# A two-layer graph network on one core: node blocks turned by transposing DMAs instead of by TensorE

## The reference

```
agg(h)  = segment_sum(h[src], dst) / max(degree, 1)
block 1:  h  = relu([h0, agg(h0)] @ W1 + b1)             # 128+128 -> 256
          y  = log_softmax([h, agg(h)] @ W2 + b2)        # 256+256 -> 128
block 2:  h3 = relu(agg(h2) @ Wl0.T + bl0 + h2 @ Wr0.T)  # 128 -> 256
          h4 = relu(agg(h3) @ Wl1.T + bl1 + h3 @ Wr1.T)  # 256 -> 256
          y  = relu(h4 @ Wa.T + ba) @ Wb.T + bb          # -> 128
```

## Time and profile before

| | |
|---|---|
| median of three runs | 587.96 us |
| the profiled execution: time / span | 587.56 us / 585.7 us |
| TensorE matmul busy | 544.2 us (93%) |
| VectorE / ScalarE busy | 225.0 / 202.9 us |
| phase 1, steps of chunks 1 to 6 | 68 to 204 us |
| phase 2 / phase 3 / phase 4 | from 204 / 276 / 372 us |
| TensorE's clock, mean over the span | 0.992 |

### The profile page before, as it was taken

How to read it: one execution, slowest core, us unless ns; L and a number is a source line. 1 busy time by engine, 2 the same in 40 slices (tenths; PEclk the granted TensorE clock), 3 DMA queues, 4 the chain that set the end, 5 groups by cost and what they waited for, 6 DMA issues and landing times.

```text
span 585.7 us, 9420 instructions
## 1 busy us (share of the span) xinstructions
PE 544.2 (93%) x3078; PEld 291.5 (50%) x3078; DVE 225.0 (38%) x500; ACT 202.9 (35%) x368; POOL 24.7 (4%) x36
## 2 busy tenths in 40 slices
PE   1367999999999999999999999999999999999996
PEld 0244655555554654445455555644545445454555
DVE  6899959577775217667411111110000001010001
ACT  1688858567664304455422222200000010100011
POOL 4410000000000000110100000000000000000000
PEclk9997999999999999999999999999999999999999
DMA  3800103010010124333121111232011212111011
GB/s 94 196 1 1 38 1 117 2 36 17 17 35 17 24 70 112 90 90 77 39 76 53 52 52 39 67 117 52 19 35 39 49 35 52 35 35 52 17 32 30
DMA packets 31372, 29.47 MB, mean 50 GB/s; under 512 B 4894, under 2 KB 30879, under 8 KB 31215
## 3 DMA queue, kind: packets, MB, share of 16 engines
q1 hardware_dynamic: 29622, 27.91, 17.6%
q10 hardware_dynamic: 1561, 0.84, 0.6%
q0 software_dynamic: 160, 0.33, 0.2%
HBM read 19.68 MB, written 9.39 MB: 50 GB/s over the span
## 4 chain that ended last, share of the span: by engine, by line
PE 87%; DVE 5%; ACT 3%; DMA 2%; issue 2%; POOL 1%; ACTq 0%; SPq 0%; DVEq 0%; POOLq 0%
PE ps L1036 54%; PE ps L1053 22%; PE ps L990 6%; PE ps L1308 2%; DVE hs_b L493 2%; PE ps L1046 1%; PE ps L1270 1%; DMA hs_b<-self_d 1%; DMA adj<-key_d,adj 1%; ACT adj L1490 1%; POOL adj L1375 1%; PE ps L1242 1%; DVE adj L1426 1%; DMA adj<-in_dst_dram 0%; ACT adj L844 0%
## 5 line engine op out<-in xcount | busy, mean ns | idle before, releaser
L1036 PE MATMUL ps<-adj,hs_b 125*128 (+2 forms) x1050 | 203.6, 351 | 0.0
L1036 PE MATMUL ps<-adj,hs_a 125*128 (+2 forms) x700 | 158.5, 353 | 0.0
L1036 PEld LDWEIGHTS ps<-adj,hs_b 125*128 125x128 f16 x1050 | 96.3, 97 | 103.9 <-issue 6.6
L493 DVE TENSOR_TENSOR hs_b<-iota,hs_b 128x1024 f16<-128x1024 f16 x150 | 95.4, 685 | 27.9 <-PE ps L990 26.9
L844 ACT ACTIVATE adj<-ps 125x500 f32 (+2 forms) x150 | 80.0, 544 | 22.8 <-PE ps L990 16.6
L990 PE MATMUL ps<-hs_b 128*128 128x125 f16 x625 | 68.5, 233 | 20.7 <-DVE hs_b L493 13.1
L990 PEld LDWEIGHTS ps<-hs_b 128*128 128x128 f16 x625 | 46.5, 103 | 65.7 <-DVE hs_b L493 34.4
L1036 PEld LDWEIGHTS ps<-adj,hs_a 125*128 125x128 f16 x700 | 58.5, 98 | 38.8 <-issue 5.4
L975 ACT ACTIVATE actT<-ps,col 128x500 f32<-128x500 f32 (+1 forms) x14 | 8.9, 633 | 148.0 <-PE ps L1053 148.0
L791 DVE TENSOR_TENSOR hs_a<-ps,hs_a 125x512 f32<-125x512 f32 (+1 forms) x7 | 4.4, 634 | 128.9 <-PE ps L1308 128.9
L1053 PE MATMUL ps<-aggT,wts 128*128 128x500 f32 (+1 forms) x112 | 44.6, 540 | 0.4 <-ACT aggT L957 0.4
(11 more groups left out here) (150 smaller groups left out, 356.4 us busy)
## 6 DMA issues: line engine op xcount, KB each, us to landing
invc<-inv_d SPq DMA_DIRECT2D x24, 250.0 KB, 3.3
h_d<-actT SPq DMA_DIRECT2D x6, 500.0 KB, 3.1
wts<-h_d SPq DMA_DIRECT2D x6, 500.0 KB, 4.0
self_d<-hs_b SPq DMA_DIRECT2D x6, 250.0 KB, 2.1
hs_b<-self_d SPq DMA_DIRECT2D x6, 250.0 KB, 3.5
hs_b<-in_x_dram SPq DMA_DIRECT2D x6, 250.0 KB
x_d<-hs_b SPq DMA_DIRECT2D x6, 250.0 KB
hs_a<-x_d SPq DMA_DIRECT2D x6, 250.0 KB
```

Of the source, the lines that this page charges most:

```text
L493: last = nc.vector.tensor_tensor(onehots[slot], iota2.unsqueeze(1).to_broadcast(shape), keys[:, ds(g * 4, 4), :].unsqueeze(2).to_broadcast ...
L1036: last = nc.tensor.matmul(acc[:, 0:n], hs[:, ds(s * (2 * w) + part * w + h * 128, 128)], adj[0:P, ds(c * (S * C) + s * n, n)], start=(isin ...
```

## The change

- Rows of the first normalization are stored to DRAM (`hs_d1`) in five pieces of 625 rows (`rows_out`), the rows of h2 chunk by chunk (`hs_d3`).
- The own rows of a full chunk come back turned: `turn_own` issues two transposing DMAs (high halves, low halves) of 512 rows x 128. VectorE adds the two (`own_sum`). `own1` and `own3` are left for chunk 6 only.
- z of a full chunk: ScalarE writes the high half as f16 (turned layout), VectorE the low half (`z_low`), SyncE stores both to `z_d`, waits, and issues four transposing DMAs of 256 rows that write `hs_b`. h3 of chunks 0 to 4 goes the same way: two ScalarE copies, two VectorE subtractions, two stores to `h16_d`, four transposing DMAs of 512 rows. `turn1` is left for chunk 6, `turn3` for chunks 5 and 6; `low` and `high` likewise.
- Phase 2 now begins on `p1_zin` (the transposed z of five chunks, of the sixth before tile 20), phase 4 on `p3_in`.
- A memset of `zT` on GpSimd, and pads zeroed on VectorE. The branch for inputs that don't fit (not taken here) gets shared semaphores.

```diff
 # SyncE
+            def turn_own(ph, c, hd, into):
+                for k in range(2):
+                    sp.dma_start_transpose(into[k], hd[ds(c * C, 512), k * D:(k + 1) * D]).then_inc(sem(f"p{ph}_hT"), 16)
             load_inv("p1_", 0, True)
+            if not slow:
+                rows_out(sp, 3, S // PIECE)          # pieces 0 to 2 are stored before the branch
+                sp.wait_ge(sem("h0_rows"), 16 * (S // PIECE))
+                turn_own(1, 0, hs_d1, turned1)
             def step1(c, full, nxt):
                 sp.wait_ge(sem("p1_agg_out"), c + 1)
                 if nxt is not None:
                     load_inv("p1_", c + 1, nxt)
                 if not slow and isinstance(c, int) and c == 0:
                     store_weights()
+                if not slow and nxt:
+                    sp.wait_ge(sem("p1_h0T"), c + 1)
+                    turn_own(1, c + 1, hs_d1, turned1)
                 sp.wait_ge(sem("p1_self"), c + 1)
                 sp.dma_start(self_d[...], selfT[...])
+                if not slow and full:
+                    sp.wait_ge(sem("p1_zlo"), c + 1)
+                    sp.dma_start(z_d[...], zboth...).then_inc(sem("p1_z_out"), 16)
+                    sp.wait_ge(sem("p1_z_out"), 16 * c + 16)
+                    for t in range(4):
+                        sp.dma_start_transpose(hs_b[...], z_d[ds(c * 256, 256), t * PT:(t + 1) * PT]).then_inc(sem("p1_zin"), 16)
...
             sp.wait_ge(sem("p2_x1_out"), 16 * NCH)
+            if not slow:
+                sp.wait_ge(sem("p2_rows"), 16 * NFULL)
+                turn_own(3, 0, hs_d3, turned3)
             sp.wait_ge(sem("p2_low"), NCH)
             load_inv("p3_", 0, True)
...
 # VectorE, phase 1
+            def own_sum(ph, c, parts):
+                dve.wait_ge(sem(f"p{ph}_hT"), 32 * c + 32)
+                wait_past(dve, "p1_h1" if ph == 1 else "p3_h3", 2 * c)
+                nc.vector.tensor_tensor(aggT[:, C:2 * C], parts[0][:, 0:C], parts[1][:, 0:C], ALU.add).then_inc(...)
                     build_b(c + 1, nxt)
                 if second:
+                    own_sum(1, 0, turned1)
                     weights_dve(dve, 0)
                     build_c(c + 1, nxt, 0, 1)
                     weights_dve(dve, 1)
                     build_c(c + 1, nxt, 1, 5)
-                else:
-                    low(c - 2, True)
-                    if nxt is not None:
-                        build_c(c + 1, nxt, 0, 5)
+                elif nxt is not None:
+                    build_c(c + 1, nxt, 0, 5)
+                if c is not NFULL:
+                    own_sum(1, c, turned1)
                 self_out(c - 1, True)
+                z_low(c - 1)
                 if nxt is not None:
                     build_c(c + 1, nxt, 5, 7)
 # VectorE, phase 3
+                if full and not slow:
+                    own_sum(3, c, turned3)
+                    if not first:
+                        low3(c - 1, True)
                 dve.wait_ge(sem("p3_inv"), 16 * c + 16)
                 dve.wait_ge(sem("p3_agg"), c + 1)
                 nc.vector.tensor_tensor(aggT[:, 0:n], bank(acc3(c, slow), n), invc[:, 0:n], ALU.mult)
-                if not first:
+                if (slow or not full) and not first:
                     low3(c - 1, True)
 # TensorE
-                own1(c - 1, True)
...
-                turn1(c - 1, True)
-            staged(3, [...], [(0, own3, 1), (8, hidden3, 1), (0, turn3, 2)], [(14, turn2, NFULL)], ...)
+            staged(3, [...], [(8, hidden3, 1)], [(14, turn2, NFULL)], ...)
```

More of the change, by code:

```diff
@@ L363, in step3 @@
                     load_inv("p3_", c + 1, nxt)
+                if not slow and nxt:
+                    sp.wait_ge(sem("p3_ownT"), c + 1)
+                    turn_own(3, c + 1, hs_d3, turned3)
                 n = width(full)
@@ L405, in sp_layers, with rows_out @@
             sp.wait_ge(sem("p4_out"), 16 * NCH)
+        def rows_out(sp, a, b):
+            for j in range(a, b):
+                sp.wait_ge(sem("n_low"), j + 1)
+                sp.dma_start(hs_d1[j * PIECE * P:(j + 1) * PIECE * P, :].rearrange("(t p) f -> p t f", p=P),
+                             tiles(ha, 2 * D)[:, j * PIECE:(j + 1) * PIECE, :]).then_inc(sem("h0_rows"), 16)
         def branch(eng, layers):
@@ L681, in dve_layers @@
                 agg_out(NFULL, False)
-                low(NFULL - 1, True)
                 self_out(NFULL, False)
@@ L883, in step1 @@
             def step1(c, full, nxt, second=False):
-                h0_turned(c - 1, True)
-                if not second:
-                    high(c - 2, True)
                 if nxt is not None:
@@ L927, in act_layers @@
                 step1(NFULL, False, None)
-                high(NFULL - 1, True)
                 whole(NFULL, False)
@@ L963, in step3 @@
                                          scale=s3[:, m:m + 1]).then_inc(sem("p3_relu"), 1)
+                if full and not slow and not (isinstance(c, int) and c == ND):
+                    act.wait_ge(sem("p3_relu"), 2 * c + 2)
+                    wait_past(act, "p3_st", 32 * c)
+                    for m in range(2):
+                        last = nc.scalar.activation(h16[0][:, m, :, 0:P], actT[:, m * C:(m + 1) * C].rearrange("p (t n) -> p t n", n=P),
+                                                    ACT.Copy)
+                    last.then_inc(sem("p3_hi"), 1)
+                    return
                 for k, (t0, t1) in enumerate(HALVES[full]):
-                    act.wait_ge(sem("p3_turned"), 2 * c + k + 1)
+                    act.wait_ge(sem("p3_turned"), 2 * c + k + 1 if slow else k + 1 if full else 3)
                     nc.scalar.activation(hs_write(hbz, c, full, 0, H)[:, t0:t1], tiles(bank(6 + k, (t1 - t0) * H, P), H),
                                          ACT.Copy).then_inc(sem("p3_high"), 1)
-            chunks(act, step3)
+            step3(0, True)
+            with act.Fori(1, ND) as c:
+                step3(c, True)
+            step3(ND, True)
+            step3(NFULL, False)
             def step4(c, full):
```

171 lines of the change are left out of this document (128 added, 43 removed).

## The result

| | before | after |
|---|---|---|
| median of four runs each, same chip | 587.98 us | 615.75 us (613.66 to 617.78) |
| the profiled execution: time / span | 587.56 / 585.7 us | 616.53 / 614.7 us |
| TensorE matmul busy | 544.2 us | 539.6 us |
| TensorE's clock, mean over the span | 0.992 | 0.974 |

What follows compares the result with a forecast made beforehand. TensorE was taken as the bound, 87% of the chain. First wait 5.0, second 7.2, clock 2.3, phase 1 1.8, phase 2 0, phase 3 1.35 made +17.65 us on 587.56: 605.2, said as 605.5 for the median; range 592 to 622.

Steps and rivals of the forecast that it cites:

- First wait: Phase 1, step 1, before count 4: VectorE waits for chunk 0's own rows turned by DMA; +5.0 us.
- Second wait: Phase 1, step 1, before count 19: chunk 1's pair of transposing DMAs is queued behind the weights' store; +7.2 us.
- Clock: Step 1: TensorE's clock falls to half after standing still, 0.7 us for the first wait, 1.6 for the second; +2.3.
- Phase 1, mid-step: Steps 2 to 5: own_sum and z_low before one-hot 19 delay count 19 by 1.2 us each; net +1.8 after 3.0 gained.
- Start of phase 3: Chunk 0's first hidden3 waits for row store, pair, own_sum and eviction; +1.25 us, the removed own3 included.
- Second boundary: Phase 3: VectorE evicts chunk 1 only after low3 of chunk 0, lengthening the chain to the next step's tile; +1.3 us.
- later ones and the step of chunk 6: Phase 3 gains: 0.2 us at each of four boundaries, 0.4 in chunk 6's step from ScalarE's copy wait; 1.2 together.
- Phase 2: z of chunk 5 through DRAM, awaited by ScalarE's z of chunk 6, is hidden by 1.5 us; cost 0.
- Start of phase 4: It begins some 9 us after the stores its first four chunks' last transposes wait for; hidden, cost 0.
- the queue of transposing DMAs is the bound: Phase 3 steps hold six; above 2.3 us each the steps wait, and other waits grow; +40, 628 and more; chance 0.11.
- only VectorE's work: Rows are turned in time everywhere, so only VectorE's added work counts; +3, 591 us; chance 0.09.
- faster: VectorE's additions fall into its idle 3.32 us, turned rows are never late, only gains stay; 5.3 off, 582.6; chance 0.06.

Runs made afterwards that it cites:

- experiment 3: Changed kernel, but VectorE sums chunk 0's own rows after the two chains of small weight operations, not before; 611.86 us.
- 8: Changed kernel with all repairs together: store and VectorE orders, split row stores, chunk 0's own rows by TensorE in phase 3, later clearing of zT; 585.31 us, ratio 0.994.
- Experiment 1: Changed kernel, but SyncE stores the turned weights after the second pair of transposing DMAs, not before it; 606.11 us.
- experiment 9: Changed kernel, but the weights' store is issued right behind the second pair, both still as late as in the changed kernel; 613.84 us.
- Experiment 5: Changed kernel, but in phase 3 chunk 0's own rows alone are turned by TensorE and copied by ScalarE again; 612.04 us.
- experiment 4: Changed kernel with every transposing DMA replaced by a plain one of the same bytes and places, so nothing is turned; 615.56 us.
- experiment 2: Changed kernel, but in steps 2 to 5 of phase 1 own rows are summed before one-hot 16 and z_low runs after one-hot 24; 611.37 us.
- experiment 10: The kernel of 8 without the clearing of zT on GpSimd; 584.65 us.
- the repaired kernels: Kernels built on the all-repairs kernel of 8, with or without zT's clearing or own rows by TensorE; 583.47 to 585.46 us.
- the best kernel: The kernel of 8 with own rows turned by TensorE everywhere, z and h3 still through DRAM, no clearing of zT; 583.47 us, ratio 0.992.
- experiment 7: Changed kernel, but each of the five stores of 625 normed rows is made in two DMAs, of 112 and 13 partitions; 614.88 us.

## Why the prediction was off by ten microseconds, and where it held

Forecast 605.5, measured 615.75: inside the range (592 to 622), outside the forecast's own (598 to 614), and on the right side. The mechanism was that of the runs; several terms were too small, and nearly all errors went the same way.

- **First wait, +5.0, measured +5.6.** Right in kind; shown by experiment 3 in part and by 8. The issue of the pair was foreseen at 71.4; it came at 73.41 in a trace that runs 1.7 later.
- **Second wait, +7.2, measured +8.3.** Experiment 1 shows the cause (order in the queue), 9 the share of the data ahead: 2 us, where I took 1. My own sign of being wrong, a pair that lands after more than 6 us, was just missed (5.85 to the sum) and met in two later kernels (7.5), but only behind the weights. The Trainium skill (DMA: Bandwidth & Descriptors, Queues, rings and completion order) says that each DMA engine takes the descriptors of one issuing engine in ring order; experiment 9 agrees: 3.8 us with the store behind the pair, against 5.3 to 7.5 with it ahead.
- **Clock, +2.3, measured +6.5.** The term that failed most. I charged 1.6 and 0.7 from one place; it was 2.8 and 1.4, and a third dip of 2.3 in phase 3 wasn't in the sum at all. It came from the wait of `hidden3` that I had put at a fourth of its length, so that error was paid twice. Experiment 5 shows how loosely it hangs: with waits of 1.15 and 2.31 us in its place the dip came one boundary later. Experiment 9 had both dips, and in experiment 4 the first wait alone cost 4.4 us of clock.
- **Phase 1, mid-step, +1.2 a step against 3.0 in all.** Count 19 waits 1.10, 1.09, 1.09 and 0.99 us in steps 2 to 5; experiment 2 shows the cause. Net +2.2 against +1.8: the steps grew by 5.1 in mid-step (4.8 said) and gained 2.9 at their starts (3.0 said), 0.5, 0.9, 0.8, 0.5 and 0.1.
- **Start of phase 3, +1.25, measured +4.2.** Three items of the chain were short: the row store took 5.3 us to the next issue (4.1 said), the pair 4.0 (3.7), and the load of inverse degrees, which I had not listed though it stands behind the pair in SyncE's order, added 1.4. This is the step that broke my own rule that a moved wait takes everything queued behind it along.
- **Second boundary +1.1 (+1.3), later ones and the step of chunk 6 -1.9 (-1.2).** Right in kind: the boundaries gave 1.3 (0.8 said), the step of chunk 6 gave 0.6 (0.4 said).
- **Phase 2, 0.** Right in kind: z of chunk 6 waited until 233.86 and `turn1` came at 234.59 without a stall.
- **Start of phase 4, 0, measured +1.9; program start, 0, measured +1.7.** Both missed. In the first I had counted the time from the stores and left out the 5.5 us that SyncE needs to issue the four transposes. Of the second, 0.7 stands already at GpSimd's first gather (11.75 us against 11.06), which experiment 10, without the clearing, has back at 11.06; 0.5 more has come by the first aggregated tile (49.69 against 48.51), and the last 0.5 is a low clock that lasted until 53.3 instead of 51.1. Beyond the gather this is scatter as much as the change: in the nine kernels that clear `zT` first, the growth up to step 1 was 0.9 to 2.1 us.
- **Slips in the sum.** By its own terms the first wait's upper bound is +8.3, not +8.7, and the second wait's lower bound +5.9, not +5.7; all bounds high, as given, make 619, not 618. The 1.3 and 0.4 us around a store's data in phase 3 stand in no row; the whole store was 5.3 us, not 4.1. Only the last moves the forecast, and it is counted above.
- **Rival "the queue of transposing DMAs is the bound"**: out. Experiment 4 takes their kind away and the time stays. The Trainium skill (Advanced Engine Details and Errata, X-Bar Transpose (TRN2)) says that such DMAs are as fast as regular ones; from issue to use the traces agree (3.9 to 4.75 us a pair, 4.4 plain). Their issue is another matter: 1.22 us of SyncE each against 0.62 to 0.75.
- **Rivals "only VectorE's work" and "faster"**: the first is excluded by the waits. The second is what the repaired kernels are: 3 to 4.7 us faster. Most of its 5.3 us of gains was there, hidden under the order of the queues; but the best kernel turns own rows on TensorE again.

Open: why the pair behind the faster stores took 5.5 us (experiment 7), and what sets how long the clock stays low.

## What to carry to other kernels

Work taken off the busiest engine is worth only what its neighbours on the path leave open: here turning 11 chunks' own rows by DMA gave nothing net, since an eviction ran under most of those matmuls and one load stayed queued behind a wait for stored rows, while turning z and h3 gave 3.5 to 4.7 us. When a step is replaced by a round trip through DRAM, write down for each place the issuing queue's order and every transfer in front and behind, and put long stores that nobody waits for last. For each such wait of TensorE add the work that then runs at the 1.2 GHz level: 1.4 to 2.8 us in the changed kernel, up to 4.4 in another execution.

## What the runs showed of the hardware that I had not expected

- A transposing DMA of 256 or 512 rows held SyncE's queue for 1.22 us (most pairs 2.43 to 2.54, fours 4.96 to 6.5), and a pair behind the 1152 KB store 3.5 to 4.05. A plain one of the same bytes took mostly 0.62 to 0.75, a plain one with long rows 0.35. From issue to use the plain pair (4.4 us) lay inside the scatter of the transposing one (3.9 to 4.75).
- Two stores of 625 rows from 125 partitions took 9.1 to 9.35 us up to the next issue, in eight kernels; split into 112 and 13 partitions, 4.9 to 5.8 us in three. The DMA engines' busy share was 0.31 in the first form and 0.88 in the second.
- VectorE's cast of 125x400 ended 0.22 or 0.23 us after the end of the GpSimd instruction (iota or memset) beside it, in all 14 traces, wherever it began: it took 0.50 us when it began 0.28 before that end, and 1.23 when it began 1.01 before. No trace has it alone. The Trainium skill (GPSIMD Engine Reference, Specifications) says that GpSimd shares its SBUF interfaces with VectorE and that some forms of VectorE instructions contend for them; the trace agrees that the two get in each other's way, and doesn't show in which form the cast ran.
